# A two-layer graph network on one core: count turns of four chunks, spread evenly between the dense products

## The chip, the cores and the metric

The kernel runs on one core of a Trainium2 chip. The metric is the device time of one execution in microseconds (us); the figure of the kernel before is the median of three runs.

## The reference

1250 nodes with 1024 features, 40000 edges, sorted by their target. A layer normalisation, two graph layers and a feed-forward block, each part added to its input:

```python
def _sage_layer(h, edge_src, edge_dst, deg_inv, W_self, W_neigh, b):
    msg = h[edge_src]
    agg = jax.ops.segment_sum(msg, edge_dst, num_segments=h.shape[0])
    mean = agg * deg_inv[:, None]
    return h @ W_self + mean @ W_neigh + b
...
dst = jnp.minimum((1250 * jax.random.uniform(..., (40000,)) ** 2.0).astype(jnp.int32), 9999)
...
h = jax.nn.relu(_sage_layer(x, ..., W_self0, W_neigh0, b0))
out = _sage_layer(h, ..., W_self1, W_neigh1, b1)
```

The targets are thus dense at the low nodes and thin at the high ones. After the graph layers `x = x + out` is normalised again and goes through `square(relu(x @ W_fc.T)) @ W_proj.T` and five steps of a threshold recurrence whose spikes are counted.

## The kernel before

**The count.** The neighbour sum is done as a matrix product: the kernel first counts, for every pair of nodes, the edges between them, into ten count tiles (`at_dram`), and multiplies with those. The 40000 edges lie in 320 chunks of 125. The 1280 padded targets are cut into 40 windows of 32; a window of index `i` counts the chunks that may hold its targets. One chunk costs one matmul of 320 columns in bf16 (L1372), between two one-hot tiles: `src_hot` (source within its tile) and `key_hot` (target within the window, and tile of the source). Windows go in the order 28 to 39, then 0 to 27 (`window_of`), and four of them make a count tile.

**Sets.** A window has a *head* of three chunks (set 0), and then *turns* of six chunks in a loop over a register range: set 1 and set 2 of three chunks each. The one-hots of the head come from GpSimd (`head_of_block`: `current` L653, then three `src_hot` L657) and VectorE (three `key_hot` L1013). Those of a turn come from VectorE (`key_one_hots`: `src_hot` of set 1 at L1022, `key_hot` of both sets at L1024) and ScalarE (`src_one_hots`: for set 2 three `dist` at L745 and one `src_hot` at L750). There is one buffer per set: its makers wait for `hot_used` of the last use.

**Steps.** The turns of a window are dealt to *steps*. `extra_turns` says, window by window, how many turns stand as steps of their own behind the first (`EXTRA_TURNS`); the last step of a window is a loop to the end of its range. Step (i, 0) has the head and one turn; step (i, j) one turn. The last step of a window ends with a 2-column matmul that closes the sum (L1388); ScalarE then copies it to the one count tile in SBUF (`copy_counts`, L762), and SyncE stores that tile after four windows (`store_counts`, L448). The first window of the next tile waits in `copy_counts` for this store (`at_stored`).

**Where steps stand.** The steps are put between the dense products of two stages of ten units each: A0 (the first pass, x times W_neigh0) and S0 (x times W_self0). A unit (`dense`) is 8 blocks k of 6 matmuls of 512 columns (L1423), 48 products, and `STEP_SLOTS` gives for each unit the blocks before which a step stands: one in A0+3, two each in A0+4 to A0+8 (blocks 3 and 6), one in A0+9, three in S0, six each in S0+1 to S0+4 and five each in S0+5 to S0+8. That makes 59 steps. On the other engines the steps of a unit stand in the order of each engine's program: VectorE makes the keys of a unit's first step at the end of the unit before; in S0 it then runs `take_self` (L1131, which takes the unit's sum out of PSUM) and after it the keys of the other steps. In A0 it runs `low_of_z`, `low_of_row`, the steps behind the first, the layer normalisation of the row tile two units on (L1032 to L1048), and the first step of the next unit. `turn_row` (L1399) transposes a normalised row tile in A0.

After S0 follow G0 (counts times z, L1507, which needs the stored count tiles), A1, S1, G1 and the feed-forward block (L1558, L1577).

Of the kernel before, what the change touches and what calls it, by code (L numbers as in the profile page):

```python
# [13 lines left out]
ds = bass.ds  # L14
# [19 lines left out]
SET = 3  # L34
HEAD_SET, LOOP_SETS = 0, (1, 2)
ACT_SET = 2
LOOP_CHUNKS = SET * len(LOOP_SETS)
# [22 lines left out]
A0_STORES = (5, 7, 9)  # L60
# [9 lines left out]
EXTRA_TURNS = {0: 8, 1: 3, 2: 2, 3: 1, 4: 1, 5: 1, 6: 1, 7: 1, 8: 1}  # L70
# [34 lines left out]
def gnn_ffn(nc, x, dst_cols, src_cols, dst_rows, w_self0, w_neigh0, b0, w_self1, w_neigh1, b1,  # L105
            w_fc, w_proj, out):
    with ExitStack() as ctx:
# [29 lines left out]
        def put_from(address, *what):  # L137
# [43 lines left out]
            ("current", [P, 2, SET], F32), ("src_hot", [P, 3, SET, 128], BF16),  # L181
            ("key_hot", [P, 3, SET, WINDOW_COLS], BF16), ("dist", [P, SET, 128], BF16))

# [200 lines left out]
        def load_ranges(engine, registers, w):  # L384

            engine.load(registers, window_range[0:1, ds(2 * w, 4)])
            values = [bass.RuntimeValue.of_register_unchecked(register, min_val=SET + end, max_val=CHUNKS + 2 + end)
# [3 lines left out]
        def turns_of_step(engine, registers, stop, i, j):  # L391
# [9 lines left out]
            latest = CHUNKS + 2 + LOOP_CHUNKS * j  # L401
            return (bass.RuntimeValue.of_register_unchecked(first, min_val=SET, max_val=latest),
                    bass.RuntimeValue.of_register_unchecked(end, min_val=SET + 1, max_val=latest + 1))

# [219 lines left out]
        def _(pool):  # L624
# [26 lines left out]
            def head_of_block(i, first, end):  # L651
                pool.wait_ge(hot_used[HEAD_SET], i + 1)
                nc.gpsimd.tensor_copy(current[:, :, :], edge_col[:, :, ds(first - SET, SET)]).then_inc(current_ready, 1)  # L653
# [39 lines left out]
        def _(act):  # L693
# [44 lines left out]
            def src_one_hots(i, j):  # L738

                first, end = turns_of_step(act, registers, stop, i, j)  # L740
                with act.Fori(first, end, LOOP_CHUNKS) as g:
                    act.wait_ge(act_hot_ready, visit)
                    for c in range(SET):
                        chunk = g + (SET * LOOP_SETS.index(ACT_SET) + c)
# [5 lines left out]
                    nc.scalar.activation(src_hot[:, ACT_SET, :, :], dist[:, :, :], ACT.Relu, bias=1.0,  # L750
# [167 lines left out]
        def _(dve):  # L918
# [34 lines left out]
            def keys_and_ranges():  # L953
# [14 lines left out]
                nc.vector.tensor_scalar(range_f[:, 0, :], ends[:, 0, :], -1.0, float(CHUNKS + SET),  # L968
                                        ALU.mult, ALU.add).then_inc(edge_steps, 1)
                dve.wait_ge(edge_steps, 18)  # L970
                nc.vector.tensor_scalar(range_f[:, 0, :], range_f[:, 0, :], float(CHUNKS + SET - 1), None,
# [684 lines left out]
```

## Time and profile before

| what | value |
|---|---|
| median of three runs | 1647.49 us (1646.90 to 1648.04) |
| the profiled execution, its own time | 1645.89 us |
| its span, first to last instruction | 1644.1 us |
| TensorE matmul busy | 1613.1 us, 98% |
| VectorE, ScalarE, GpSimd busy | 908.7, 469.1, 100.2 us |
| count matmuls L1372 | 474, 78.9 us busy |
| steps | 59, between about 59 us and 316 us of the span |

Busy time of a matmul is modelled from its start to its end, and successive ones overlap; what one costs on the engine is read from start to start. "Idle before" names what ended the wait of an engine.

### The profile page before, as it was taken

To read this page: it belongs to the slowest core of one execution; us is meant where nothing else is said; L and a number is where in the kernel's file an instruction comes from. 1 tells how busy PE (TensorE), PEld (TensorE's weight loads), DVE (VectorE), ACT (ScalarE), POOL (GpSimd) and SP (SyncE) were. 2 spreads that over 40 slices of the span, in tenths; PEclk is the share of its full clock that TensorE was granted. 3 is DMA by queue.
4 is the path that set the end of the run, shared out by engine and by line. 5 is a ranking of instruction groups with operands and counts; after the bars stand their busy time and mean duration, and the time that the engine had idled before them with its cause. 6 is when DMAs were issued, how large, how long until landed. Compare 5 with 4: busy or idle time off the path is not lost.

```text
span 1644.1 us, 22526 instructions
## 1 busy us (share of the span) xinstructions
PE 1613.1 (98%) x7764; PEld 1350.8 (82%) x7767; DVE 908.7 (55%) x1700; ACT 469.1 (29%) x830; POOL 100.2 (6%) x190
## 2 busy tenths in 40 slices
PE   7999999999999999999999999999999999999997
PEld 6777666688888888889899898998998888888884
DVE  7776778556311312556344343343443788888868
ACT  3344555311111100114032131231321333333358
POOL 0122135300000000001000000000001000000000
PEclk9999999999999999999999999999999999999998
DMA  8222233357522553657221120220213233333321
GB/s 295 114 107 93 84 133 135 141 210 275 216 102 77 208 198 130 217 188 253 114 88 52 50 102 26 77 77 30 98 51 128 103 115 115 115 115 115 116 90 49
DMA packets 55927, 205.45 MB, mean 125 GB/s; under 512 B 5330, under 2 KB 13852, under 8 KB 50340
## 3 DMA queue, kind: packets, MB, share of 16 engines
q1 hardware_dynamic: 53524, 191.76, 32.6%
q0 software_dynamic: 2320, 12.58, 2.0%
q8 instruction: 52, 0.85, 0.2%
q14 instruction: 31, 0.25, 0.0%
HBM read 153.85 MB, written 50.47 MB: 124 GB/s over the span
## 4 chain that ended last, share of the span: by engine, by line
PE 91%; DVE 4%; issue 2%; DMA 1%; ACT 1%; DVEq 0%; POOL 0%; SPq 0%; ACTq 0%; POOLq 0%
PE bank L1558 26%; PE bank L1423 25%; PE bank L1577 24%; PE bank L1507 11%; PE bank L1372 3%; PE bank L1399 2%; DVE key_hot L1024 1%; ACT spikes L898 0%; DVE lif_a L1330 0%; DMA at_dram<-counts_tile 0%; DVE w L1077 0%; DVE src_hot L1022 0%; DVE lif_c L1324 0%; DMA w_landing<-w_self 0%; DVE y L1289 0%
## 5 line engine op out<-in xcount | busy, mean ns | idle before, releaser
L1423 PE MATMUL bank<-w,xt 128*128 128x512 f32 x1920 | 458.8, 395 | 2.6 <-DVE w L1077 2.6
L1558 PE MATMUL bank<-x2t,fc_w 128*128 128x384 f32 (+1 forms) x2304 | 438.4, 350 | 0.5 <-ACT relu L863 0.5
L1558 PEld LDWEIGHTS bank<-x2t,fc_w 128*128 128x128 f32 x2304 | 411.7, 188 | 25.7 <-issue 0.8
L1423 PEld LDWEIGHTS bank<-w,xt 128*128 128x128 f32 x1920 | 357.7, 189 | 76.9 <-issue 3.0
L1577 PE MATMUL bank<-pr_w,hid 128*128 128x512 f32 (+1 forms) x1824 | 418.7, 390 | 0.0
L1577 PEld LDWEIGHTS bank<-pr_w,hid 128*128 128x128 f32 (+1 forms) x1824 | 338.1, 185 | 75.5
L1289 DVE TENSOR_TENSOR y<-y,bank 128x512 f32<-128x512 f32 (+1 forms) x152 | 104.2, 686 | 215.2 <-PE bank L1577 215.2
L1507 PE MATMUL bank<-z,at 128*128 128x512 f32 x800 | 187.0, 392 | 0.0
L1507 PEld LDWEIGHTS bank<-z,at 128*128 128x128 f32 x800 | 148.8, 188 | 30.2
L858 ACT ACTIVATE pr_w<-pr_raw 128x1024 fp32r<-128x1024 f32 x64 | 67.1, 1049 | 366.1 <-PE bank L1577 363.0
L1232 DVE TENSOR_TENSOR square<-relu 128x384 f32<-128x384 f32 (+1 forms) x96 | 56.8, 592 | 143.3 <-ACT relu L863 143.2
L863 ACT ACTIVATE relu<-bank 128x384 f32<-128x384 f32 (+1 forms) x96 | 49.9, 519 | 227.6 <-PE bank L1558 227.6
L1024 DVE TENSOR_SCALAR key_hot<-iota,edge_col 125x320 bf16<-125x320 f16 x354 | 94.7, 308 | 0.3 <-PE bank L1372 0.3
L1372 PE MATMUL bank<-key_hot,src_hot 125*128 125x320 bf16 x474 | 78.9, 302 | 9.1 <-DVE key_hot L1024 2.7
L1214 DVE TENSOR_TENSOR fc_w<-fc_raw,fc_w 128x1024 fp32r<-128x1024 f32 x64 | 78.2, 1222 | 9.1 <-ACT fc_w L853 8.0
L1226 DVE TENSOR_TENSOR pr_w<-pr_raw,pr_w 128x1024 fp32r<-128x1024 f32 x64 | 78.0, 1218 | 1.6 <-ACT pr_w L858 1.6
L1372 PEld LDWEIGHTS bank<-key_hot,src_hot 125*128 125x128 bf16 x474 | 39.5, 98 | 46.6 <-issue 24.9
L657 POOL TENSOR_SCALAR src_hot<-iota,current 125x128 bf16<-125x128 f16 x120 | 73.8, 627 | 8.1 <-POOL current L653 8.1
L1131 DVE TENSOR_TENSOR rows<-bank,bias 128x1024 f32<-128x1024 f32 x20 | 24.5, 1223 | 88.2 <-PE bank L1423 88.2
L1071 DVE TENSOR_TENSOR z<-bank,z 128x1024 fp32r<-128x1024 f32 x20 | 24.4, 1222 | 87.7 <-ACT z L723 87.5
L853 ACT ACTIVATE fc_w<-fc_raw 128x1024 fp32r<-128x1024 f32 x63 | 65.8, 1045 | 1.1 <-DMA fc_raw<-w_fc 1.1
L745 ACT ACTIVATE dist<-iota,edge_col 125x128 bf16<-125x128 f16 x177 | 58.0, 391 | 7.1 <-issue 2.8
(127 smaller groups left out, 914.1 us busy)
## 6 DMA issues: line engine op xcount, KB each, us to landing
fc_raw<-w_fc SPq DMA_DIRECT2D x64, 512.0 KB, 4.4
pr_raw<-w_proj SPq DMA_DIRECT2D x64, 512.0 KB, 3.5
xt<-xt_dram SPq DMA_DIRECT2D x24, 1024.0 KB, 5.0
xt_dram<-xt SPq DMA_DIRECT2D x18, 1024.0 KB, 4.4
at<-at_dram SPq DMA_DIRECT2D x20, 640.0 KB, 5.5
part_dram<-rows SPq DMA_DIRECT2D x20, 512.0 KB, 4.0
rows<-part_dram SPq DMA_DIRECT2D x20, 512.0 KB, 4.2
rows<-x SPq DMA_DIRECT2D x18, 512.0 KB, 5.1
```

What stands on the lines that cost most here:

```text
L657: ins = nc.gpsimd.tensor_scalar(src_hot[:, HEAD_SET, c, :], iota[0:P, 0:128], current[:, 0, c:c + 1], None, ALU.is_equal)
L853: nc.scalar.activation(fc_w[:, q, :, HI, :], fc_raw[:, q, :, :], ACT.Copy).then_inc(fc_high, 1)
L858: nc.scalar.activation(pr_of(j)[:, HI, :], pr_raw[:, j % 2, :], ACT.Copy).then_inc(pr_high, 1)
L1024: ins = nc.vector.tensor_scalar(key_hot[:, s, c, :], iota[0:P, :], float(v * WINDOW_COLS), edge_col[:, 1, ds(chunk, 1)], ALU.add, ALU.is_e ...
L1214: nc.vector.tensor_tensor(fc_w[:, q, :, LO, :], fc_raw[:, q, :, :], fc_w[:, q, :, HI, :].bitcast(F32), ALU.subtract).then_inc(fc_low, 1)
L1226: nc.vector.tensor_tensor(pr_of(j)[:, LO, :], pr_raw[:, j % 2, :], pr_of(j)[:, HI, :].bitcast(F32), ALU.subtract).then_inc(pr_low, 1)
L1289: nc.vector.tensor_tensor(part, part, bank[0:height, 2 * (n % 2) + q, :], ALU.add).then_inc(y_added, 1)
L1372: ins = nc.tensor.matmul(bank[:, 4 + i % 2, 0:WINDOW_COLS], src_hot[:, s, c, :], key_hot[:, s, c, :], start=(start and c == 0), stop=False)
L1423: ins = nc.tensor.matmul(bank[:, 2 * (u % 2) + q, :], xt[j][:, a, k, :], w[:, k, b, q * HALF:(q + 1) * HALF], start=(k == 0 and m == 0), s ...
L1507: ins = nc.tensor.matmul(bank[:, 2 * (u % 2) + q, :], left[j][:, s, :], right.bitcast(F32) if exact else right, start=(s == 0 and b == HI) ...
L1558: ins = nc.tensor.matmul(bank[:, 4 + (c if g == 0 else j % 2), 0:n], fc_w[:, j % 2, k, a, :], x2t[g][:, k, v, c0:c0 + n], start=(k == 0 an ...
L1577: ins = nc.tensor.matmul(bank[0:height, 2 * (n % 2) + q, :], hid_of(g, j)[:, a, n * T:n * T + height], pr_of(j)[:, v, q * HALF:(q + 1) * H ...
```

## The change

A turn has four chunks instead of six: sets 1 and 2 hold two chunks each, the head still three. `EXTRA_TURNS` is drawn up again, window by window: 34 extra turns instead of 19, so 74 steps instead of 59. Steps may stand before any of the 48 products of a unit, not only before a block, and are spread evenly: A0+4 to A0+8 hold three each from product 14 on (12 products apart), A0+9 one, S0 three (products 30, 36, 42, as before), S0+1 to S0+5 and S0+8 seven each, S0+6 and S0+7 six each. SyncE stores count tile 2 in its program for unit A0+8 instead of A0+9. `ACT.Relu` at L750 works on two chunks. Line numbers behind L1000 shift by two (L1024 becomes L1026, L1372 becomes L1374, L1423 becomes L1425).

```diff
-SET = 3
+HEAD_CHUNKS, LOOP_SET = 3, 2
 HEAD_SET, LOOP_SETS = 0, (1, 2)
 ACT_SET = 2
-LOOP_CHUNKS = SET * len(LOOP_SETS)
+LOOP_CHUNKS = LOOP_SET * len(LOOP_SETS)
...
-A0_STORES = (5, 7, 9)
+A0_STORES = (5, 7, 8)
...
-EXTRA_TURNS = {0: 8, 1: 3, 2: 2, 3: 1, 4: 1, 5: 1, 6: 1, 7: 1, 8: 1}
+EXTRA_TURNS = dict(enumerate((12, 4, 3, 2, 2, 1, 2, 1, 1, 1, 1, 1, 1, 1))) | {18: 1}
...
-for _unit, _ks in ([(A0 + 3, (5,))] + [(A0 + n, (3, 6)) for n in range(4, TILES - 1)] + [(A0 + 9, (2,)), (S0, (5, 6, 7))]
-                   + [(S0 + p, (0, 1, 2, 4, 5, 6)) for p in range(1, 5)] + [(S0 + p, (0, 2, 3, 5, 6)) for p in range(5, 9)]):
-    STEP_SLOTS[_unit] = list(zip(_ks, TURNS[_count:]))
-    _count += len(STEP_SLOTS[_unit])
+for _unit, _steps, _from, _products in (
+        [(A0 + 3, 1, 30, 12)] + [(A0 + n, 3, 14, 36) for n in range(4, TILES - 1)] + [(A0 + 9, 1, 12, 12), (S0, 3, 30, 18)]
+        + [(S0 + p, 6 if p in (6, 7) else 7, 0, 48) for p in range(1, 9)]):
+    STEP_SLOTS[_unit] = [(_from + _products * m // _steps, turn) for m, turn in enumerate(TURNS[_count:_count + _steps])]
+    _count += _steps
...
-                    for c in range(SET):
-                        chunk = g + (SET * LOOP_SETS.index(ACT_SET) + c)
+                    for c in range(LOOP_SET):
+                        chunk = g + (LOOP_SET * LOOP_SETS.index(ACT_SET) + c)
...
-                for c in range(SET):
+                for c in range(HEAD_CHUNKS if s == HEAD_SET else LOOP_SET):
                     ins = nc.tensor.matmul(bank[:, 4 + i % 2, 0:WINDOW_COLS], src_hot[:, s, c, :], key_hot[:, s, c, :],
                                            start=(start and c == 0), stop=False)
...
                 for k in range(KD):
-                    if between is not None and k in between:
-                        between[k]()
                     if p == 0:
                         pe.wait_ge(w_low, w_lows(phase, k))
                     for m, (a, b) in enumerate(PASSES):
                         for q in range(2):
+                            for other in between.get(2 * (len(PASSES) * k + m) + q, ()):
+                                other()
...
-                dense(S0, p, {k: (lambda step=step: step_of_edges(*step)) for k, step in STEP_SLOTS.get(S0 + p, [])})
+                dense(S0, p, products_between(S0 + p))
```

**Matrix engine, unit A0+4**, from its first step on; `xt,w` are its 48 dense products, `ident,rows` a turned row tile, `key_hot,src_hot` the count. Before:

```order
L1423 MATMUL bank<-w,xt_67 128x512 x12
L1372 MATMUL bank<-key_hot,src_hot 128x320 x3
L1382 UNCONDITIONAL_BRANCH
L1372 MATMUL bank<-key_hot,src_hot 128x320 x6
L1385 ISA
L1382 COMPARE_AND_BRANCH
L1388 MATMUL bank<-iota,zero_w 128x2
L1423 MATMUL bank<-w,xt_67 128x512 x18
```

Now:

```order
L1425 MATMUL bank<-w,xt_67 128x512 x8
L1374 MATMUL bank<-key_hot,src_hot 128x320 x3
L1384 UNCONDITIONAL_BRANCH
L1374 MATMUL bank<-key_hot,src_hot 128x320 x4
L1387 ISA
L1384 COMPARE_AND_BRANCH
L1390 MATMUL bank<-iota,zero_w 128x2
L1425 MATMUL bank<-w,xt_67 128x512 x12
```

A step has seven count matmuls instead of nine, and 12 dense products follow it instead of 18.

**Matrix engine, the last steps of the count**, in unit S0+8; the last row is all of unit S0+9. Before:

```order
L1423 MATMUL bank<-w,xt_67 128x512 x6
L1372 MATMUL bank<-key_hot,src_hot 128x320 x3
L1382 UNCONDITIONAL_BRANCH
L1372 MATMUL bank<-key_hot,src_hot 128x320 x6
L1385 ISA
L1382 COMPARE_AND_BRANCH
L1388 MATMUL bank<-iota,zero_w 128x2
L1423 MATMUL bank<-w,xt_67 128x512 x12
L1423 MATMUL bank<-w,xt_68 128x512 x48
```

Now:

```order
L1425 MATMUL bank<-w,xt_67 128x512 x7
L1374 MATMUL bank<-key_hot,src_hot 128x320 x3
L1384 UNCONDITIONAL_BRANCH
L1374 MATMUL bank<-key_hot,src_hot 128x320 x4
L1387 ISA
L1384 COMPARE_AND_BRANCH
L1390 MATMUL bank<-iota,zero_w 128x2
L1425 MATMUL bank<-w,xt_67 128x512 x7
L1425 MATMUL bank<-w,xt_68 128x512 x48
```

The gaps between steps, 6 and 12 products in turn before, are 6 or 7 each, and the last step stands 55 instead of 60 products ahead of the end of S0.

## Rows read from the trace of the kernel before

**Rows 1.** the page, busy time, share of the span and instructions of each engine

```profile
PE 1613.1 (98%) x7764; PEld 1350.8 (82%) x7767; DVE 908.7 (55%) x1700; ACT 469.1 (29%) x830; POOL 100.2 (6%) x190
```

**Rows 2.** groups by line: engine, operation, count, busy us, mean ns, idle before

```profile
L1372 PE MATMUL bank<-key_hot,src_hot 125*128 125x320 bf16 x474 | 78.9, 302 | 9.1 <-DVE key_hot L1024 2.7 <-ACT src_hot L750 2.3 <-DVE key_hot L1013 1.7
```

**Rows 3.** matrix engine in time: start, us, line, tiles, count; full steps, two gaps

```profile
261.40 2.99 PE L1423 MATMUL bank<-w,xt 128*128 128x512 f32 x12
264.24 1.40 PE L1372 MATMUL bank<-key_hot,src_hot 125*128 125x320 bf16 x9
265.47 0.17 PE L1388 MATMUL bank<-iota,zero_w 125*128 125x2 f16 x1
265.50 1.63 PE L1423 MATMUL bank<-w,xt 128*128 128x512 f32 x6
267.24 1.72 PE L1372 MATMUL bank<-key_hot,src_hot 125*128 125x320 bf16 x9
```

**Rows 4.** matrix engine in time, steps without a head

```profile
165.85 1.04 PE L1372 MATMUL bank<-key_hot,src_hot 125*128 125x320 bf16 x6
...
168.09 1.07 PE L1372 MATMUL bank<-key_hot,src_hot 125*128 125x320 bf16 x6
```

**Rows 5.** matrix engine in time, from the last step of the count on

```profile
316.06 13.87 PE L1423 MATMUL bank<-w,xt 128*128 128x512 f32 x60
329.76 6.52 PE L1507 MATMUL bank<-z,at 128*128 128x512 f32 x28
```

**Rows 6.** all engines in time, GpSimd's work for the next head

```profile
264.99 0.19 POOL L653 COPY current<-edge_col 125x6 f32 x1 [1.70 <-PE bank L1372]
...
265.38 1.76 POOL L657 TENSOR_SCALAR src_hot<-iota,current 125x128 bf16<-125x128 f16 x3 [0.20 <-POOL current L653]
```

**Rows 7.** all engines in time, the same at the start of unit S0+8

```profile
298.01 1.40 PE L1372 MATMUL bank<-key_hot,src_hot 125*128 125x320 bf16 x9
...
298.20 1.23 DVE L1131 TENSOR_TENSOR rows<-bank,bias 128x1024 f32<-128x1024 f32 x1 [0.49 <-PE bank L1423]
...
299.16 1.99 POOL L657 TENSOR_SCALAR src_hot<-iota,current 125x128 bf16<-125x128 f16 x3 [0.20 <-POOL current L653]
```

**Rows 8.** matrix engine in time, unit S0+0

```profile
158.44 0.57 PE L1372 MATMUL bank<-key_hot,src_hot 125*128 125x320 bf16 x3 [1.71 <-DVE key_hot L1013]
159.48 0.58 PE L1372 MATMUL bank<-key_hot,src_hot 125*128 125x320 bf16 x3 [0.47 <-DVE key_hot L1024]
160.24 0.57 PE L1372 MATMUL bank<-key_hot,src_hot 125*128 125x320 bf16 x3 [0.18 <-DVE key_hot L1024]
160.54 2.80 PE L1423 MATMUL bank<-w,xt 128*128 128x512 f32 x6
163.14 1.48 PE L1372 MATMUL bank<-key_hot,src_hot 125*128 125x320 bf16 x6
```

**Rows 9.** stretches: us, busy time by engine, granted clock, DMA share, GB/s

```profile
95.33:109.85 14.52, 14.52 (x77) 11.49 (x76) 10.80 (x39) 6.14 (x15) 3.89 (x8) 1.00 0.25 97
264.24:283.17 18.93, 18.41 (x100) 12.85 (x99) 15.95 (x61) 9.39 (x25) 10.23 (x20) 1.00 0.34 118
161.00:163.00 2.00, 2.00 (x6) 1.32 (x4) 1.17 (x6) 1.42 (x4) 1.07 (x2) 0.50 0.00 0
```

**Rows 10.** all engines in time, a unit of the first pass

```profile
107.49 0.82 DVE L1048 TENSOR_SCALAR rows<-rows,mean_var,rstd 128x1024 f32<-128x1024 f32 x1
...
109.85 0.82 PE L1399 MATMUL bank<-ident,rows 128*128 128x128 f32 x6
```

**Rows 11.** DMA issues of the count tile: count, KB, us to landing

```profile
at_dram<-counts_tile SPq DMA_DIRECT2D x10, 640.0 KB, 3.1
```

**Rows 12.** the store issued at 299.9 us, its time to landing

```profile
DMA to landing us min/median/max: 6.3/6.3/6.3
```

**Rows 13.** what waited on that store, all engines in time

```profile
306.25 0.44 ACT L762 ACTIVATE counts_tile<-bank 128x320 f32<-128x320 f32 x1 [4.66 <-DMA at_dram<-counts_tile]
...
308.17 0.58 PE L1372 MATMUL bank<-key_hot,src_hot 125*128 125x320 bf16 x3 [2.06 <-ACT src_hot L750]
```

More of the change, by code:

```diff
@@ L180, in gnn_ffn @@
             ("edge_col", [P, 2, CHUNKS + PAD_CHUNKS], F32), ("iota", [128, WINDOW_COLS], F16), ("zero_w", [P, T], F16),
-            ("current", [P, 2, SET], F32), ("src_hot", [P, 3, SET, 128], BF16),
-            ("key_hot", [P, 3, SET, WINDOW_COLS], BF16), ("dist", [P, SET, 128], BF16))
+            ("current", [P, 2, HEAD_CHUNKS], F32), ("src_hot", [P, 3, max(HEAD_CHUNKS, LOOP_SET), 128], BF16),
+            ("key_hot", [P, 3, max(HEAD_CHUNKS, LOOP_SET), WINDOW_COLS], BF16), ("dist", [P, LOOP_SET, 128], BF16))
         (edge_int, tmp_int, key_part, dst_int, dst_rows_f, chunk_min, chunk_max, group_min, group_max, window_first,
@@ L652, in head_of_block @@
                 pool.wait_ge(hot_used[HEAD_SET], i + 1)
-                nc.gpsimd.tensor_copy(current[:, :, :], edge_col[:, :, ds(first - SET, SET)]).then_inc(current_ready, 1)
+                nc.gpsimd.tensor_copy(current[:, :, :], edge_col[:, :, ds(first - HEAD_CHUNKS, HEAD_CHUNKS)]).then_inc(current_ready, 1)
                 pool.wait_ge(current_ready, i + 1)
                 pool.sem_inc(current_seen, 1)
-                for c in range(SET):
+                for c in range(HEAD_CHUNKS):
                     ins = nc.gpsimd.tensor_scalar(src_hot[:, HEAD_SET, c, :], iota[0:P, 0:128], current[:, 0, c:c + 1],
@@ L749, in src_one_hots @@
                     act.wait_ge(hot_used[ACT_SET], visit)
-                    nc.scalar.activation(src_hot[:, ACT_SET, :, :], dist[:, :, :], ACT.Relu, bias=1.0,
+                    nc.scalar.activation(src_hot[:, ACT_SET, 0:LOOP_SET, :], dist[:, :, :], ACT.Relu, bias=1.0,
                                          scale=-1.0).then_inc(act_hot_ready, 1)
@@ L1011, in key_one_hots @@
                     dve.wait_ge(current_ready, i + 1)
-                    for c in range(SET):
+                    for c in range(HEAD_CHUNKS):
                         ins = nc.vector.tensor_scalar(key_hot[:, HEAD_SET, c, :], iota[0:P, :], float(v * WINDOW_COLS),
@@ L1018, in key_one_hots @@
                         dve.wait_ge(hot_used[s], visit)
-                        for c in range(SET):
-                            chunk = g + (SET * place + c)
+                        for c in range(LOOP_SET):
+                            chunk = g + (LOOP_SET * place + c)
                             if s != ACT_SET:
@@ L1401, in turn_row, with dense @@
                     ins.then_inc(row_turned, 1)
-            def dense(stage, p, between=None):
+            def dense(stage, p, between={}):
                 u, phase, n = stage + p, PHASE[stage], ORDER[stage][p]
@@ L1476, in _, with products_between @@
             turn_row(0, 0)
-            dense(A0, 0, {4: lambda: turn_row(0, 1)})
-            for n in range(1, TILES):
-                between = {k: (lambda step=step: step_of_edges(*step)) for k, step in STEP_SLOTS.get(A0 + n, [])}
-                if n + 1 < TILES:
-                    between[1 if n > 2 else 2] = lambda: turn_row(0, n + 1)
-                if n == 2:
-                    between[0], between[5] = turn_bounds, spread_bounds
-                if n == 3:
-                    between[0] = sum_held
+            def products_between(unit, *others):
+                between = {}
+                for place, other in others:
+                    between.setdefault(place, []).append(other)
+                for place, step in STEP_SLOTS.get(unit, []):
+                    between.setdefault(place, []).append(lambda step=step: step_of_edges(*step))
+                return between
+            dense(A0, 0, {24: [lambda: turn_row(0, 1)]})
+            for n in range(1, TILES):
+                others = []
+                if n == 2:
+                    others += [(0, turn_bounds), (30, spread_bounds)]
+                if n == 3:
+                    others += [(0, sum_held)]
+                if n + 1 < TILES:
+                    others += [(6 if n > 2 else 12, lambda: turn_row(0, n + 1))]
                 if n == 4:
@@ L1489, in _ @@
                     few_edges = pe.value_load(many_int[0:1, 1:2], min_val=0, max_val=1)
[L1490 removed]
+                dense(A0, n, products_between(A0 + n, *others))
             for p in range(TILES):
[L1492 removed]
+                dense(S0, p, products_between(S0 + p))
             def degree(n):
@@ L1531, in _ @@
                 aggregate(0, n)
-            dense(A1, 0, {1: lambda: turn_row(1, TILES - 1)})
+            dense(A1, 0, {6: [lambda: turn_row(1, TILES - 1)]})
             for p in range(1, TILES):
```

15 lines of the change are left out of this document (7 added, 8 removed).

## The prediction

> **What bounds the kernel now.** I read the busy times first. The matrix engine is busy 98% of the span [rows 1], so a change in the count is worth what it takes off that engine, as products or as waits; other engines matter only where it waits for them. The group of the count's matmuls [rows 2] shows 474 of them (59 steps x 6 + 40 heads x 3) and 9.1 us of idle time before them, released by key one-hots of VectorE and `src_hot` of ScalarE. The engine in time then gives the prices. Nine count products take 265.47 - 264.24 = 1.23 us, **0.137 us** each [rows 3]; 60 dense products take 13.70 us, **0.228** each [rows 5]. Twelve dense products behind a full step take 2.84 instead of 2.74 us, and the closing product 0.03, so closing a window costs 0.13 [rows 3]. A step without a head and the six dense products behind it take 168.09 - 165.85 = 2.24 us, where the products alone come to 6 x 0.137 + 6 x 0.228 = 2.19 [rows 4]: the loop around it costs 0.05.
>
> **Where it waits.** From the start of S0+1 (168.09, [rows 4]) to the end of the last step (316.06, [rows 5]) are 147.97 us. In them stand 372 dense products (84.9 us), 345 count products (47.3) and 28 closings (3.6), 135.8 in all, so **12.1 us are waits**. A pair of full steps shows what they are: behind a long gap the second follows without delay, behind a gap of six products it starts 267.24 - 265.50 = 1.74 us later where six products need 1.37 + 0.1, and is itself stretched from 1.40 to 1.72 us [rows 3]. That is 0.27 + 0.32, some 0.58 us for each short gap between heads. Its cause is GpSimd: it copies `current` 0.75 us after the step begins, starts the three `src_hot` 0.39 later and needs 1.76 for them [rows 6], so the next head can't start before 0.75 + 0.39 + 1.76 + 0.1 = **3.01 us** (267.24 - 264.24 is 3.00). At a unit's start `take_self` runs first on VectorE and GpSimd's work ends at 301.15, 3.14 us behind the step's start of 298.01 [rows 7]: 3.25 us with the handover. One wait of another kind, 2.06 us, is ScalarE's `src_hot`, held up because the copy of the sum before it waited for the store of the only count tile [rows 13].
>
> **The change, part by part.**
>
> *Count products.* 74 turns of four and 40 heads of three are 416 instead of 474: each of the 74 steps turns its loop once (by the edges of the sorted targets, worked out window by window; before, 59 steps made 59 turns, as the 474 matmuls of [rows 2] confirm). 58 x 0.137 = **-7.95 us**. VectorE loses 58 key and 29 source one-hots, ScalarE 29 `dist`; they are off the path except as waits, below. Closings stay 40.
>
> *First pass.* A0+4 to A0+6 have three full steps instead of two, 21 count products instead of 18, which is inside the sum above. New waits there: a unit takes 14.52 us now with VectorE busy 10.80 [rows 9]. An operation of VectorE's in a step costs 0.245 us there: (15.95 - 1.23 for `take_self`) / 60 in a unit of five steps of twelve [rows 7, 9]. Three steps of nine come to 6.6 us for two of twelve at 5.9, so a unit will take some 15.0 with VectorE near 11.5. Steps are then 12 x 0.228 + 0.96 + 0.13 = 3.83 us apart, against GpSimd's 3.01. The normalised row tile must be there at product 6: now it is ready at 108.31, 1.5 us ahead of its use at 109.85 [rows 10]. Behind the last step of a unit, whose copy ScalarE makes ahead of the normalisation's root, stand 10 products instead of 12, so the margin falls to about 1.0 us, still hidden; if it is gone, five units lose what is missing. Window i = 8 follows i = 7 within a unit, and its copy waits for the store of tile 1, issued while a 1 MB transfer runs: I put 0.3 us.
>
> *Unit S0+0.* The engine waits 1.71 + 0.47 + 0.18 us at its first step [rows 8], because VectorE reaches its keys only behind the eight weight parts. That step has no head any more (window 12's moved to A0+7), so four operations for set 1 stand ahead of the first product instead of three for the head, at most 0.245 us more, but set 2 follows sooner: I take waits of 1.8 + 0.1 us, **-0.45 us**. Behind the waits the granted clock is 0.50 [rows 9], the 1.2 GHz level: six dense products take 163.14 - 160.54 = 2.60 us instead of 1.48, and the next step loses 0.37 more, 1.5 in all. The engine now rests 1.9 us instead of 2.36 there, about as long as the 2.06 us of [rows 13]; the six dense products of [rows 3] have the same pace long before and the sixty of [rows 5] just behind that wait, so the clock stayed at its full level, 2.4 GHz, there. I expect it to hold: **-1.5 us**, a little better than even.
>
> *Steps of S0+1 to S0+8.* 54 steps, 6 or 7 products apart. What now waits:
> - Head behind head at 7 products: 7 x 0.137 + 0.13 + 1.60 = 2.69 us against 3.01, 0.32 x 5 in S0+8, and 0.8 at its start, where 6 products stand: 3.25 - (1.09 + 1.37). Together 2.4.
> - Head behind head at 8 products (S0+6, S0+7): 2.92 against 3.01, five times 0.1, and 0.3 at a unit's start: 0.8.
> - Unit starts with a step without a head first: `take_self` (1.23 us, [rows 7]) stands ahead of the keys of the second step. S0+1 and S0+2: 0.3 each. S0+4 and S0+5, where the second step has a head: 0.65 each. S0+3: 0.1. Together 2.0.
> - In the middle of units most heads alternate with a step without one. Two gaps pass (about 4.8 us) and VectorE needs 15 x 0.245 = 3.7 for both. None.
> - The count tile's store: windows come quicker, 2.7 to 3.0 us apart at the end. A store of 3.1 us [rows 11] gives a copy in time; the one issued behind an `xt` load took 6.3 [rows 12]. In the change that window's store falls behind the load, in S0+8; i = 28 is the exposed one: 0.4.
>
> Together 5.6, with A0's 0.3 5.9 instead of 12.1: **-6.2 us**. The unit starts and the 3.01 are the best known of these; the ends for the whole item are no waits at all (-12.1) and all that are there today (0).
>
> *End of S0.* The last step stands 5 products (1.1 us) nearer the end. Its store (some 3 us, [rows 11]) would have landed 9 us ahead of the first G0 product [rows 5]; the issue of the `at` loads goes by `take_self` of S0+8, whose place doesn't move. Nothing. A1, S1, G1 and the feed-forward block are as before.
>
> Sum: -7.95 - 0.45 - 1.5 - 6.2 = **-16.1 us**. The sum is against the profiled execution, 1645.89 us by its own time (1644.1 span), which would become 1629.8. The median of the runs is 1.6 us above it, so I predict **1631.4 us**.
>
> *A rule against it.* The rows show that the sequencer of the matrix engine runs ahead: 15 more loops cost at most 15 x 0.05 = 0.8 us [rows 4], and I leave it in the range. The Trainium skill, page "Advanced Engine Details and Errata", section "Control Flow Timing", gives some 51 ns for a branch and 108 ns for a compare-and-branch. By that page 15 steps more would add about 2.4 us if nothing hid them. The trace agrees only in that a loop isn't free.
>
> **The rivals.**
> 1. *The clock falls again in S0+0.* All else as forecast: 1631.4 + 1.5 = 1632.9 us. For it: the rest is still 1.9 us. Against: 2.06 us were borne elsewhere [rows 13].
> 2. *The waits don't fall.* The gaps of 12 products, behind which no step waited, are gone; if VectorE (15.95 of 18.93 us busy in such a unit, [rows 9]) answers late at every gap, the waits stay near 12: 1631.4 + 6.2 = 1637.6, with the clock's 1.5 1639.1.
> 3. *Branches on the path.* Each of 15 loops costs between 0.05 us, as in [rows 4], and, uncovered, three times that: +0.8 to +2.3 us, 1632.2 to 1633.7. The page above gives about the upper end.
> 4. *Slower: every short gap costs what it costs today between heads.* 54 steps x 0.58 = 31 us of waits instead of 5.6: 1631.4 + 25.7 = 1657.1 us. It decides from 0.45 us for each step on, where the 16.1 + 3.3 us are used up. For it: [rows 3]. Against: [rows 4], where a step without a head stands six products behind another without that loss, and 34 of the 74 steps have no head.
> 5. *The change doesn't do what it says:* a window's loop turns twice in its last step because the table is short; each such turn adds 4 x 0.137 and a wait of some 1.8 us. Five of them would give 1643. The windows' edges speak against it.
>
> **How the numbers follow.** Forecast 40%, rival 1 27%, rival 2 19%, rival 3 7%, rival 4 3%, rival 5 1%, and 3% for a first pass that starts to wait by 1 us or more in each unit (1636 or more). 0.2% (3.3 us) is about what a measurement of this kernel can tell from no change. The range runs from 1626.5 (waits down to 1 us instead of 5.9) to 1639.0 (rival 2 with the clock's loss). Outside it lie rivals 4 and 5, half of the slow first pass, and the sizes I have misjudged altogether. Rival 4 is the slower case; a first pass that waits 2.5 us in each unit is within 0.2%. **Faster by over 0.2%: 0.94; within 0.2%: 0.03; slower: 0.03.**
>
> **What would show it.** 416 count matmuls. From the start of S0+1 to the last step's end some 136 us, with 377 dense products, instead of 148 with 372. Head pairs in S0+8 3.0 us apart, released by GpSimd. Units of the first pass with three full steps near 15.0 us and no idle time. Granted clock 1.0 behind S0+0. The forecast is wrong if VectorE's keys release most steps, if units A0+5 to A0+7 take over 15.3 us, or if ScalarE's copies wait for `at_dram` and the matrix engine behind them.

## The result and the profile after

The changed kernel takes **1631.9 us** (median of four runs, 1630.89 to 1632.4) against 1647.2 us beside it (four runs); the ratio is 0.9903, 95% interval 0.9891 to 0.9915. That is 15.3 us, about 1%, less. The forecast was 1631.4. The profiled execution took 1631.58 us with a span of 1629.6, 14.5 less than the span of before.

The page's busy times (columns as in [rows 1]):

```profile
PE 1603.5 (98%) x7709; PEld 1344.4 (83%) x7709; DVE 894.4 (55%) x1613; ACT 462.8 (28%) x816; POOL 97.9 (6%) x190
```

The group of the count's matmuls among the groups by line (columns as in [rows 2]):

```profile
L1374 PE MATMUL bank<-key_hot,src_hot 125*128 125x320 bf16 x416 | 71.0, 301 | 4.6 <-DVE key_hot L1026 2.2 <-POOL src_hot L659 0.6 <-issue 0.5
```

The count has 416 matmuls, as worked out, so every step turned its loop once. Idle time before them fell from 9.1 to 4.6 us, and GpSimd now stands among its causes.

**The first pass.** All engines in time, from the last steps of a unit to the next:

```profile
107.32 1.13 PE L1374 MATMUL bank<-key_hot,src_hot 125*128 125x320 bf16 x7
...
108.31 3.90 PE L1425 MATMUL bank<-w,xt 128*128 128x512 f32 x16
...
110.06 0.81 DVE L1050 TENSOR_SCALAR rows<-rows,mean_var,rstd 128x1024 f32<-128x1024 f32 x1
...
112.06 1.03 PE L1401 MATMUL bank<-ident,rows 128*128 128x128 f32 x8
```

and one stretch of it and two of S0, the last in S0+0 (columns as in [rows 9]):

```profile
96.96:112.06 15.10, 15.10 (x82) 11.73 (x81) 12.01 (x41) 6.85 (x17) 5.87 (x12) 1.00 0.34 138
283.88:303.10 19.22, 17.79 (x97) 12.04 (x98) 15.66 (x57) 8.95 (x24) 11.95 (x24) 1.00 0.33 118
161.00:163.00 2.00, 2.00 (x12) 1.45 (x11) 1.01 (x7) 1.09 (x4) 0.00 (x0) 1.00 0.00 0
```

A unit with three full steps takes 15.10 us and the matrix engine is busy all of it. The row tile is ready at 110.87, 1.2 us ahead of its use; before it was 1.5 [rows 10].

**Unit S0+0**, the matrix engine in time:

```profile
159.58 0.95 PE L1374 MATMUL bank<-key_hot,src_hot 125*128 125x320 bf16 x4 [1.98 <-DVE key_hot L1026]
160.36 1.63 PE L1425 MATMUL bank<-w,xt 128*128 128x512 f32 x6
161.83 0.72 PE L1374 MATMUL bank<-key_hot,src_hot 125*128 125x320 bf16 x4
```

Six products take 1.47 us behind the rest, where they took 2.60 [rows 8], and the granted clock in the third stretch above is 1.00 instead of 0.50.

**The start of unit S0+2**, where the first two steps have no head; all engines in time:

```profile
181.76 0.72 PE L1374 MATMUL bank<-key_hot,src_hot 125*128 125x320 bf16 x4
181.96 1.23 DVE L1133 TENSOR_TENSOR rows<-bank,bias 128x1024 f32<-128x1024 f32 x1 [0.49 <-PE bank L1425]
...
183.99 0.95 PE L1374 MATMUL bank<-key_hot,src_hot 125*128 125x320 bf16 x4
```

**Unit S0+8**, where every step has a head; all engines in time:

```profile
283.88 1.11 PE L1374 MATMUL bank<-key_hot,src_hot 125*128 125x320 bf16 x7
...
285.01 1.98 POOL L659 TENSOR_SCALAR src_hot<-iota,current 125x128 bf16<-125x128 f16 x3 [0.20 <-POOL current L655]
...
287.08 1.11 PE L1374 MATMUL bank<-key_hot,src_hot 125*128 125x320 bf16 x7 [0.59 <-POOL src_hot L659]
...
290.08 1.11 PE L1374 MATMUL bank<-key_hot,src_hot 125*128 125x320 bf16 x7 [0.16 <-issue]
```

The matrix engine in time, the first step of S0+1, the last dense products behind the last step, and the first of G0:

```profile
165.71 0.72 PE L1374 MATMUL bank<-key_hot,src_hot 125*128 125x320 bf16 x4
...
303.10 12.74 PE L1425 MATMUL bank<-w,xt 128*128 128x512 f32 x55
315.68 6.52 PE L1518 MATMUL bank<-z,at 128*128 128x512 f32 x28
```

Behind the first step of a unit the next head comes after 3.20 us, and the matrix engine waits for GpSimd's one-hots; then heads stand 3.00 apart. From the start of S0+1 (165.71) to the end of the last step (303.10) are 137.39 us, with 377 dense products (86.1), 297 count products (40.7) and 28 closings (3.6): 130.4 us of work and **7.0 us of waits**, where there were 12.1. Measured the same way, 3.2 of the 7.0 lie in S0+6 to S0+8 (53.57 us from 249.53 to 303.10, with 50.4 of work), where heads follow heads, and 3.5 at the starts of S0+1 to S0+5.

**Where the time went**, on the landmarks of the two profiles: the first step of the count starts 0.8 us *later* than before (60.23 against 59.45), in a part of the kernel that the change leaves as it was. In the first unit of A0 24 dense products take longer in this execution, and all of the shift is there:

```profile
12.99 8.59 PE L1425 MATMUL bank<-w,xt 128*128 128x512 f32 x24 [2.64 <-DVE w L1079]
```

(7.76 before.) The first product of G0 starts 14.1 us earlier (315.68 against 329.76), so the count gained 14.9; another 0.4 us of the 14.5 lies behind it. The terms: -7.95 for 58 count products, -1.5 for the clock, -5.1 for waits in S0+1 to S0+8, and -0.15 for the rest in S0+0 make 14.7.

### The profile page after: what moved, and what is told of

It reads as the page before. It is cut to its first block, busy times and chain, and to the rows that moved or that the text cites. A ratio compares the mean times of both kernels' runs of the same rounds, so it can differ in the third digit from the quotient of the medians.

```text
span 1629.6 us, 22403 instructions
## 1 busy us (share of the span) xinstructions
PE 1603.5 (98%) x7709; PEld 1344.4 (83%) x7709; DVE 894.4 (55%) x1613; ACT 462.8 (28%) x816; POOL 97.9 (6%) x190
## 4 chain that ended last, share of the span: by engine, by line
PE 95%; issue 1%; DVE 1%; DMA 1%; ACT 1%; DVEq 0%; POOL 0%; SPq 0%; ACTq 0%; POOLq 0%
PE bank L1588 26%; PE bank L1569 26%; PE bank L1425 26%; PE bank L1518 11%; PE bank L1374 3%; PE bank L1401 2%; ACT spikes L900 1%; PE bank L1620 0%; DMA w_landing<-w_self 0%; DVE w L1079 0%; DMA pr_raw<-w_proj 0%; DMA at_dram<-counts_tile 0%; DMA rows<-x 0%; DVE key_hot L1026 0%; DVE xt L1067 0%
## 5 line engine op out<-in xcount | busy, mean ns | idle before, releaser
L1425 PE MATMUL bank<-w,xt 128*128 128x512 f32 x1920 | 462.7, 396 | 2.6 <-DVE w L1079 2.6
L1425 PEld LDWEIGHTS bank<-w,xt 128*128 128x128 f32 x1920 | 356.8, 189 | 76.9 <-issue 3.3
L1026 DVE TENSOR_SCALAR key_hot<-iota,edge_col 125x320 bf16<-125x320 f16 x296 | 81.4, 316 | 0.5 <-issue 0.2
L1374 PE MATMUL bank<-key_hot,src_hot 125*128 125x320 bf16 x416 | 71.0, 301 | 4.6 <-DVE key_hot L1026 2.2
L1374 PEld LDWEIGHTS bank<-key_hot,src_hot 125*128 125x128 bf16 x416 | 34.0, 98 | 39.0 <-issue 23.6
L717 ACT ACTIVATE xt<-bank 128x512 fp32r<-128x512 f32 x48 | 26.2, 596 | 117.4 <-PE bank L1401 117.4
```

The lines of the kernel that those rows point to most:

```text
L1026: ins = nc.vector.tensor_scalar(key_hot[:, s, c, :], iota[0:P, :], float(v * WINDOW_COLS), edge_col[:, 1, ds(chunk, 1)], ALU.add, ALU.is_e ...
L1374: ins = nc.tensor.matmul(bank[:, 4 + i % 2, 0:WINDOW_COLS], src_hot[:, s, c, :], key_hot[:, s, c, :], start=(start and c == 0), stop=False)
L1425: ins = nc.tensor.matmul(bank[:, 2 * (u % 2) + q, :], xt[j][:, a, k, :], w[:, k, b, q * HALF:(q + 1) * HALF], start=(k == 0 and m == 0), s ...
```

## The experiments

Each is the changed kernel with an edit, run four or five times beside the kernel before (medians of 1647.2 to 1647.6 us). Differences are to the 1631.9 us of the change. Where a profile is read, "the S0 part" is the time from the first step of S0+1 to the end of the last step: 137.39 us in the change.

**e1: six chunks, spread evenly.** The old turns and the old number of steps, spread evenly as the change does; SyncE stores count tile 2 in A0+9 again.

```diff
-HEAD_CHUNKS, LOOP_SET = 3, 2
+HEAD_CHUNKS, LOOP_SET = 3, 3
-EXTRA_TURNS = dict(enumerate((12, 4, 3, 2, 2, 1, 2, 1, 1, 1, 1, 1, 1, 1))) | {18: 1}
+EXTRA_TURNS = {0: 8, 1: 3, 2: 2, 3: 1, 4: 1, 5: 1, 6: 1, 7: 1, 8: 1}
-        [(A0 + 3, 1, 30, 12)] + [(A0 + n, 3, 14, 36) for n in range(4, TILES - 1)] + ...
-        + [(S0 + p, 6 if p in (6, 7) else 7, 0, 48) for p in range(1, 9)]):
+        [(A0 + 3, 1, 30, 12)] + [(A0 + n, 2, 18, 36) for n in range(4, TILES - 1)] + ...
+        + [(S0 + p, 6 if p < 5 else 5, 0, 48) for p in range(1, 9)]):
```

> The changed kernel's code with turns of six chunks and the old extra turns (59 steps, two in each unit of the first pass), but spread evenly: 8 products apart in S0+1 to S0+4, 9 or 10 apart in S0+5 to S0+8. It keeps all 474 count matmuls, and the head of window 12 in S0+0. Theory (the waits come from short gaps between heads, GpSimd's chain of 3.01 us): full steps 9.6 products apart stand 3.55 us apart, so nearly all of the 12.1 us of waits go but for unit starts and the one store: 2.5 stay, the clock falls as before. 1647.2 - 9.6 = 1637.6 us, 1636.5 to 1639.5. Rival (VectorE's longer turns of nine operations are late at any even spacing, and only turns of four chunks help): waits stay near 10, 1645 us or more.

Measured: 1640.59 us (1639.42 to 1641.48). Above the range by 1 us, and far from the rival. All engines in time, unit S0+8:

```profile
293.69 0.39 SPq L450 DMA_DIRECT2D at_dram<-counts_tile  x1
...
300.72 0.44 ACT L764 ACTIVATE counts_tile<-bank 128x320 f32<-128x320 f32 x1 [5.37 <-DMA at_dram<-counts_tile]
...
302.63 0.58 PE L1374 MATMUL bank<-key_hot,src_hot 125*128 125x320 bf16 x3 [2.83 <-ACT src_hot L752]
```

From S0+1's first step at 168.88 to the last step's end at 310.16 are 141.28 us with 136.3 of work: 5.0 us of waits, and 2.83 of them are this one. The store of a count tile is issued 1.7 us behind the load of an x tile and lands 7 us later; the copy of window 36 waits for it on ScalarE, and the source one-hots behind the copy come late. Without it the waits are 2.2 us, as expected. So spreading takes away the waits of short gaps also for turns of six; I had forgotten that the wider steps put window 35 at the very start of the unit.

**e8: the same with the store first.** SyncE issues the store of tile 8 ahead of the two transfers.

```diff
+                if p == 8:
+                    store_counts(8)
                 if p + 1 < TILES and p >= 1:
                     load_xt(S0, p + 1)
...
-                    if i % PER_TILE == PER_TILE - 1 and ... :
+                    if i % PER_TILE == PER_TILE - 1 and ... and (p, i) != (8, 35):
```

> The first experiment (turns of six chunks, spread evenly) with the store of count tile 8 issued ahead of the load of the next x tile and of the part store in unit S0+8, instead of behind them. Theory (the 2.83 us wait of the matrix engine in the last unit is the copy of window 36, which waits for that store, slow because two transfers run ahead of it): the store lands in some 3.5 us instead of 7 and the wait goes or shrinks below 0.5: 1640.6 - 2.6 = 1638.0 us, 1637.2 to 1639. Rival (ScalarE is late there for other reasons): 1640.6 as before.

Measured: 1636.36 us (1634.64 to 1636.93), 4.2 less than e1 and below the range; the wait at 302.63 is gone. That is more than the wait itself. The five executions lie in two groups, 1634.6 and 1634.9, and 1636.4 to 1636.9. The profiled one is of the first group, and its S0+0 has no lower clock, while the profiled execution of e1 has it. Between these two profiles the S0 part falls from 141.28 to 138.19 us (1.9 of waits are left), and what stands ahead of it, from the first step of the count on, from 109.01 to 107.06, by the clock and a rest that is 0.4 shorter. The three of the second group are 3.7 to 4.2 us below e1's median. The mechanism stands; why the medians differ by 1 us more than the S0 part does, I can't place.

**e2: blocks of six only.** Same steps, but none stands within a block.

```diff
+for _unit, _places in (
+        [(A0 + 3, (30,))] + [(A0 + n, (12, 24, 36)) for n in range(4, TILES - 1)] + [(A0 + 9, (12,)), (S0, (30, 36, 42))]
+        + [(S0 + p, (0, 6, 12, 24, 30, 36) if p in (6, 7) else (0, 6, 12, 18, 24, 30, 36)) for p in range(1, 9)]):
+    STEP_SLOTS[_unit] = list(zip(_places, TURNS[_count:]))
+    _count += len(_places)
```

> The changed kernel with its 74 steps put before blocks of six products only: products 12, 24, 36 in the first pass, 0, 6, 12, 18, 24, 30, 36 (or 0, 6, 12, 24, 30, 36) in S0+1 to S0+8. Theory: head behind head at six products waits 3.01 - 2.46 = 0.55 us instead of 0.32 at seven and 0.1 at eight; about 10 such gaps, 3 of them now with 12 products; the first pass unchanged. About 2 us more than the changed kernel, 1634 us, 1632.8 to 1635.5. Rival (places of single products matter for every step): 5 us or more, 1637 and up. Rival (it is the size of the turns alone): 1632, no difference.

Measured: 1633.96 us (1633.46 to 1634.59), 2.1 more than the change: as the theory had it. The matrix engine in time, S0+8:

```profile
288.83 1.11 PE L1374 MATMUL bank<-key_hot,src_hot 125*128 125x320 bf16 x7 [0.60 <-POOL src_hot L659]
...
291.82 1.11 PE L1374 MATMUL bank<-key_hot,src_hot 125*128 125x320 bf16 x7 [0.38 <-issue]
```

Heads are 2.99 us apart at six products as they are 3.00 apart at seven: the places don't set their distance, and each product between them only moves work under the wait. The S0 part takes 139.62 us, 2.2 more than in the change.

**e3: two steps in a unit of the first pass.**

```diff
-        [(A0 + 3, 1, 30, 12)] + [(A0 + n, 3, 14, 36) for n in range(4, TILES - 1)] + ...
-        + [(S0 + p, 6 if p in (6, 7) else 7, 0, 48) for p in range(1, 9)]):
+        [(A0 + 3, 1, 30, 12)] + [(A0 + n, 2, 18, 36) for n in range(4, TILES - 1)] + ...
+        + [(S0 + p, 8 if p in (1, 7, 8) else 7, 0, 48) for p in range(1, 9)]):
```

> The changed kernel with two steps instead of three in each unit of the first pass; the five others go to S0, whose units S0+1, S0+7 and S0+8 hold eight, six products apart. The work is the same. Theory: the first pass has no waits either way; in S0+7 and S0+8 some 14 heads follow one another at six products, 0.55 us each instead of 0.3, and the head of window 12 is back in S0+0, where the rest before the first step and perhaps the clock's fall return. 4 to 7 us more than the changed kernel: 1637 us, 1635 to 1639. Rival (the first pass is already full, a third step there costs what it saves in S0): no difference, 1632.

Measured: 1636.78 us (1635.38 to 1637.71), 4.9 more, in the middle of the range. SyncE stores count tile 2 in A0+9 here too. In the profile the waits of the S0 part are 10.9 us instead of 7.0, twelve pairs of heads at six products with 0.53 to 0.56 each among them, and the clock did not fall. The third step in the first pass is worth that much at equal work: there GpSimd's chain fits between steps, and the steps of S0 get more room.

**e4: the head's third source one-hot on VectorE.**

```diff
-                for c in range(HEAD_CHUNKS):
+                for c in range(HEAD_CHUNKS - 1):
                     ins = nc.gpsimd.tensor_scalar(src_hot[:, HEAD_SET, c, :], ...)
...
+                    c = HEAD_CHUNKS - 1
+                    ins = nc.vector.tensor_scalar(src_hot[:, HEAD_SET, c, :], iota[0:P, 0:128], current[:, 0, c:c + 1],
+                                                  None, ALU.is_equal)
                     ins.then_inc(key_hot_ready[HEAD_SET], 1)
```

> The changed kernel with GpSimd making two of the head's three source one-hots and VectorE the third, behind the head's keys. Theory (GpSimd's chain sets 3.0 us between heads): the chain falls by 0.59 us, so the pairs of heads in S0+6 to S0+8 no longer wait for it; VectorE, with 2.5 us for a full step, fits in 2.69. The waits fall by 2 us, 1630 us, 1629 to 1631. Rival (VectorE is as late as GpSimd there): unchanged or up to 1 us slower, 1632 to 1633.

Measured: **1628.74 us** (1628.1 to 1629.17), 3.2 less than the change, better than the range. The count's matmuls and two heads of S0+8, in time:

```profile
L1377 PE MATMUL bank<-key_hot,src_hot 125*128 125x320 bf16 x416 | 71.4, 301 | 3.2 <-DVE key_hot L1029 1.8 <-DVE src_hot L1018 0.3
```

```profile
288.23 1.13 PE L1377 MATMUL bank<-key_hot,src_hot 125*128 125x320 bf16 x7
...
290.92 1.20 PE L1377 MATMUL bank<-key_hot,src_hot 125*128 125x320 bf16 x7
```

These two are 2.69 us apart, what the products between them take, and no release by GpSimd is left. But VectorE, which has the operation now, is late in its turn: the six distances between heads from the start of S0+8 on are 2.66 (six products), 3.12, 2.69, 2.75, 2.70 and 2.75 us. The worst of them, in time:

```profile
285.11 1.58 PE L1377 MATMUL bank<-key_hot,src_hot 125*128 125x320 bf16 x7
...
285.39 0.72 DVE L1029 TENSOR_SCALAR key_hot<-iota,edge_col 125x320 bf16<-125x320 f16 x3
```

From the first step of S0+6 to the last step's end are 51.28 us instead of 53.57, so 2.3 us less: there are 0.9 us of waits instead of 3.2. The S0 part falls by 2.15 us, and the two profiles differ by another 0.65 at the kernel's start, where the edit does nothing. The theory's 2 us are thus what the trace shows; the rest of the 3.2 isn't shown to come from the edit.

**e9: a fourth on GpSimd.** The opposite: one more operation behind the three, written to an unused part of `src_hot`.

```diff
+                ins = nc.gpsimd.tensor_scalar(src_hot[:, 1, 2, :], iota[0:P, 0:128], current[:, 0, c:c + 1],
+                                              None, ALU.is_equal)
                 ins.then_inc(src_hot_ready, 1)
```

> The changed kernel with a fourth source one-hot on GpSimd behind each head's three, written where nothing reads it. Theory (GpSimd's chain sets the distance of heads): the chain grows by 0.59 us to 3.6; heads that follow heads wait that much more in S0+6 to S0+8, some 13 times; the first pass, 3.83 us apart, still doesn't wait. 1631.9 + 7.5 = 1639.4 us, 1638 to 1641, and pairs 3.6 us apart in S0+8. Rival (VectorE's keys are as late as GpSimd's, as good as nothing hangs on GpSimd alone): 1632 to 1634.

Measured: 1637.26 us (1636.92 to 1637.92), 5.4 more; the range began at 1638. The matrix engine in S0+8:

```profile
293.20 1.11 PE L1376 MATMUL bank<-key_hot,src_hot 125*128 125x320 bf16 x7 [0.74 <-issue]
...
296.79 1.11 PE L1376 MATMUL bank<-key_hot,src_hot 125*128 125x320 bf16 x7 [0.75 <-issue]
```

Heads are 3.59 us apart, 0.59 more than with three. Twelve heads follow heads in S0+6 to S0+8 (I had put 13), and from the first step of S0+6 to the last step's end are 60.17 us, 6.6 more, close to 12 x 0.59 = 7.1. The median shows less; in the profiled execution the rest in S0+0 was 0.7 us shorter and the start 0.4 us earlier. VectorE has the same operations here as in the change, so the distance is GpSimd's doing.

**e5: S0+0's steps earlier and later.**

```diff
-        ... [(A0 + 9, 1, 12, 12), (S0, 3, 30, 18)]
+        ... [(A0 + 9, 3, 12, 36), (S0, 1, 42, 6)]
```

> The changed kernel with three steps in A0+9 (products 12, 24, 36) and one in S0+0 (product 42) instead of one and three. The work is the same. Theory (the 2.2 us of rest in S0+0 come from a step that stands before VectorE has finished the eight weight parts, while the product at 42 has to wait for the last part anyway): the matrix engine reaches product 42 later than the keys are there, the rest goes and no other takes its place: 2 us less than the changed kernel, 1629.9 us, 1629.2 to 1631. Rival (the weight parts set the time of S0+0, and the rest moves to product 42): 1631.5 to 1632.5. Rival (two more steps on VectorE in A0+9 make the first parts late): 1632.5 or more.

Measured: **1628.58 us** (1628.36 to 1628.82), 3.3 less than the change and below the range. The rest is gone, and no other came; the matrix engine in time, from A0+9 on:

```profile
148.46 12.53 PE L1425 MATMUL bank<-w,xt 128*128 128x512 f32 x54
160.83 0.72 PE L1374 MATMUL bank<-key_hot,src_hot 125*128 125x320 bf16 x4
```

54 products take 12.37 us, 0.229 each: the weight parts arrive in time. Between the two profiles the part ahead of S0+1, from the first step of the count on, is 2.45 us shorter (103.03 against 105.48), the S0 part is the same (137.44), and 0.5 us are the kernel's start. So the rest explains some 2.4 of the 3.3 us; the remainder isn't shown to come from the edit.

**e7: a longer rest in S0+0.** Four more one-hots on VectorE ahead of the first keys (step (12, 5), set 1), into unused parts of the tiles.

```diff
+                            if (i, j, s) == (12, 5, 1):
+                                nc.vector.tensor_scalar(key_hot[:, 1 + c, 2, :], ...)
+                                nc.vector.tensor_scalar(src_hot[:, 1 + c, 2, :], ...)
```

> The changed kernel with four more one-hots on VectorE ahead of the first keys in S0+0, written where nothing reads them, some 0.8 us. Theory (the clock fell in the kernel before because the engine rested 2.4 us around that step, and no longer falls with 2.0): a rest of 2.7 to 2.8 us brings the lower clock back behind it, so it costs 0.8 + 1.5 = 2.3 us, 1634.2 us, and the profile shows a stretch at 0.50. Rival (the fall has to do with the head's products or the clock's own phase, not with the rest): 0.8 us, 1632.7, no stretch at 0.50.

Measured: 1632.48 us (1631.35 to 1633.61), 0.6 more. The matrix engine in time:

```profile
159.07 1.21 PE L1379 MATMUL bank<-key_hot,src_hot 125*128 125x320 bf16 x4 [1.90 <-DVE key_hot L1031]
159.87 2.96 PE L1430 MATMUL bank<-w,xt 128*128 128x512 f32 x6
162.63 0.82 PE L1379 MATMUL bank<-key_hot,src_hot 125*128 125x320 bf16 x4
```

The rest was *not* longer: the weight parts were done earlier in this execution (VectorE reached the four operations at 157.43, and the keys of the changed kernel at 158.69), which took back what the four cost. And yet the clock fell: six products took 2.76 us. The median lies at the rival's 1632.7, but the profile has the lower clock that the rival denies, and not the longer rest of the theory. Neither was tested as it was meant.

**e10: a still longer rest.** Four reductions of 0.4 us each in the same place.

```diff
+                        if (i, j, s) == (12, 5, 1):
+                            for half in range(4):
+                                nc.vector.tensor_reduce(key_hot[0:P, 1, 2, half:half + 1],
+                                                        edge_col[:, half % 2, 0:CHUNKS], AX.X, ALU.max)
```

> The changed kernel with four reductions on VectorE ahead of the first keys in S0+0, some 1.6 us, whose results nothing reads. Theory (a long enough rest always brings the lower clock): the rest is 3.3 to 3.8 us in every execution, the stretch at 0.50 is there and costs 1.5 us: 1631.9 + 1.6 + 1.5 = 1635.0 us or somewhat less where executions of the changed kernel had a fall already, 1634 to 1635.5, and all executions lie close together. Rival (the fall comes and goes whatever the rest): two groups 1.5 us apart, median 1633.5 to 1635.

Measured: 1633.58 us (1632.62 to 1635.15), 1.7 more. That is below the theory's range and inside the rival's, without the rival's two groups. The matrix engine in time, and two stretches:

```profile
160.55 1.25 PE L1378 MATMUL bank<-key_hot,src_hot 125*128 125x320 bf16 x4 [3.38 <-DVE key_hot L1030]
161.39 2.60 PE L1429 MATMUL bank<-w,xt 128*128 128x512 f32 x6
```

```profile
158.00:160.00 2.00, 0.00 (x0) 0.00 (x0) 2.00 (x7) 0.69 (x2) 0.00 (x0) 1.00 0.00 0
160.00:162.00 2.00, 1.45 (x5) 0.91 (x6) 1.50 (x9) 0.10 (x1) 0.00 (x0) 0.50 0.00 0
```

The granted clock is 0.50 in all of the second stretch, and the first product of the step starts at 160.55, so the lower clock began while the engine still rested and lay partly under the rest. The six products lost 1.0 us (161.39 to 163.83, where 1.47 is the full pace), against 1.5 us in before for six products and the step behind them.

**e6: e4 and e5 together.**

> The run before this together with the head's third source one-hot on VectorE. Both take away different waits, so their gains should add up: 1628.7 - 2.0 = 1626.7 us, 1626 to 1628, with the count's matmuls waiting for less than 1.5 us in all. Rival (VectorE, which bears both, becomes the bound in S0+1): 1628 to 1629.

Measured: **1626.5 us** (1626.23 to 1626.61), ratio to the kernel before 0.9871 (0.9856 to 0.9886). 5.4 us below the change, where the medians of its parts add up to 3.2 + 3.3 = 6.5. Its profile has the two gains as its parts' profiles show them: 2.4 us ahead of S0+1, and 2.1 in the S0 part (135.32 us). The group of the count's matmuls:

```profile
L1377 PE MATMUL bank<-key_hot,src_hot 125*128 125x320 bf16 x416 | 71.2, 301 | 1.3 <-DVE src_hot L1018 0.3
```

## Why the prediction was right

**The sum.** The median came out 0.5 us from the forecast, and part of that is luck. By the profiles the count gained 14.9 us against 16.1 forecast. The profiled execution was to take 1629.8 us and took 1631.58, 1.8 more: 1.2 for the terms below and the rest mainly for its late start. The median hides this, because I put it 1.6 us above the profiled execution, as in before, and it lies only 0.3 above.

**Count products: right.** 416, and 58 x 0.137 = 7.95 us rests on a count and on a duration that the trace shows unchanged (0.137 a product, 0.96 us from the start of a step of seven to its closing). It is the one term that I left without an experiment.

**GpSimd's chain: right, and shown in both directions.** 3.00 us between heads in the change, 3.59 with one operation more, and 2.69, the products' own time, with one less where VectorE is in time. I had priced the remaining waits in S0+6 to S0+8 at 3.2 us, and 3.2 are there. That e4's median is 3.2 us lower, too, is a coincidence: its profile gains 2.3 us there, since 0.9 of waits stay with VectorE.

**The price of a short gap: right in size, half wrong in cause.** I put both parts of the 0.27 + 0.32 us down to GpSimd. The second, the stretched step, is VectorE's, which makes the last keys of the step while the step runs. In the trace of before, all engines in time:

```profile
267.31 0.93 DVE L1024 TENSOR_SCALAR key_hot<-iota,edge_col 125x320 bf16<-125x320 f16 x4
```

It has twelve one-hots to make for a step with a head there, and nine in the change. With nine the steps of e2 aren't stretched even at six products (1.11 us at 291.82). So the smaller turns do take something off a short gap that spacing alone doesn't. In the sum this did no harm, because I had priced the pairs of the change by the 3.01 us alone.

**The first pass: right.** 15.10 us a unit with no idle, margin 1.2 us where I put 1.0. e3 gives the worth of the third step there, 4.9 us. The 0.3 us for window 8's copy did not appear.

**Unit starts: mis-sized.** I put 2.0 us for the five that begin with a step without a head or with the head of a longer window. Measured against their products, the first two steps of S0+1, S0+2 and S0+3 lose some 0.65 us each and those of S0+4 and S0+5 0.78, 3.5 us in all. The step that failed is that I priced the delay of the second step's first matmul (183.99 - 181.76 = 2.23 us, where 1.92 is the work: 0.3) and forgot that the step is stretched too, because set 2 comes after set 1 from the same engine: 0.95 instead of 0.72 us. With these 1.5 us the waits are 7.0 instead of 5.6.

**The rest in S0+0: less gained.** 1.98 + 0.23 instead of 1.8 + 0.1. e7's VectorE was done with the weight parts 1.26 us earlier than the change's, 0.4 of it by the kernel's start, and e9's rest was 1.25 us, so this wait is not known to better than some 0.8 us.

**The clock: the outcome came, the reason doesn't hold.** I argued that 1.9 us of rest would be borne because 2.06 us elsewhere had been [rows 13]. The runs deny such a bound:

| profile | rest at the first step of S0+0 | clock behind it |
|---|---|---|
| before | 1.71 + 0.47 + 0.18 | 0.50 |
| e1 | 2.01 + 0.47 + 0.18 | 0.50 |
| e8 | 1.64 + 0.47 + 0.18 | 1.00 |
| e7 | 1.90, then a stretched step | 0.50 |
| change | 1.98, then a stretched step | 1.00 |
| e2, e4 | 1.81, 1.79 | 1.00 |
| e3 | 1.66, then a stretched step | 1.00 |
| e9 | 1.25, then a stretched step | 1.00 |
| e10 | 3.38 | 0.50, from within the rest |

With rests of about 2 us it falls in some executions and not in others; a rest of 2.3 was borne and one of 1.9 was not. That it held in the profiled execution was luck as far as my reason goes. A chance of 27% for a new fall was fair for one execution (e7 fell; change, e2 and e4, with about the same rest, did not), but then the term -1.5 should have been a share of it, for the median too. What decides in one execution stays open; none of these runs tells it. Whether the median of the change holds executions of either kind isn't shown: only the profiled one shows its clock in detail.

**The rivals.** The clock did not fall in the profiled execution (rival 1). Even spreading did not leave the waits where they were (rival 2): 7.0 us, not 12. Nor did every short gap cost what it costs between heads (rival 4): these 7.0 us are all the waits of 54 steps six to eight products apart. No loop turned twice (rival 5): 416 matmuls. Fifteen loops more cost next to nothing (rival 3): a step without a head and the seven products behind it take 2.17 us in the middle of S0+1, where 4 x 0.137 + 7 x 0.228 = 2.14. Here the rule of the Trainium skill, "Advanced Engine Details and Errata", section "Control Flow Timing" (51 ns for a branch, 108 ns for a compare-and-branch), names a cost that the trace doesn't find on the path of the matrix engine.

**What the change gives back.** e8 and the change are the same count with turns of six and of four. The change saves 7.95 us of products. In the profiles it gives 5.1 of them back as waits in S0+1 to S0+8, 7.0 us against 1.9: 3.2 because the shorter steps brought heads 2.7 us together, below what GpSimd can follow, and most of the rest at the unit starts. From the first step of the count to G0 it is 3.1 us faster (255.45 against 258.51). The medians differ by 4.5 (1636.36 and 1631.9); the profiled execution of e8 is of its faster group, and what the others lost isn't shown.

## What to carry to other kernels

When work is interleaved into a full engine, write down for each kind of step how soon its slowest helper can serve the next one; space the steps at least that far, and first fill places where they are that far apart anyway. Shrinking the steps themselves shortens that distance, so the helper's chain must shrink with them: moving one short operation from GpSimd to VectorE gained a fifth of what the whole change had, by the medians. It may then be the next helper that is late, as VectorE was in e4. And a step that has to wait for a late producer should stand behind the product that waits for the same producer.

## What the hardware showed beside this

- **One GpSimd one-hot of 125 x 128 is worth 0.59 us in the chain, the same on VectorE 0.16 to 0.29** (1.76 us for three; start to start on VectorE, the longer value while GpSimd works).
- **The first dense unit scatters and can shift the whole kernel.** Its 24 products took 7.18 us (e7) to 8.62 us (e3) in these profiles. Up to 8.24 us this moved nothing: the first step of the count started at 59.58 to 59.90 us. In the change and in e3 (8.59 and 8.62) it started at 60.23 and 60.27, in before (7.76) at 59.45. The granted clock is 1.00 there in every profile; what makes the difference stays open.
- **The executions of one kernel scatter by 0.4 to 2.5 us.** e5 and e6, which have no rest in S0+0, lie within 0.5 and 0.4 us; with the rest it is 1.0 to 1.1 in e2, e4 and e9, 1.5 in the change, and 2.1 to 2.5 in e1, e3, e7, e8 and e10. A clock that falls in some executions only would do this, but no profile shows both kinds for one kernel.
